# Gated attention block: the second norm's output is kept in natural layout, and turned and quantised from PSUM in the first barrier

## What is computed

```python
x = x + tanh(g_xattn) * attention(layernorm(x), ctx, ctx)      # causal scores, softmax over the query axis
y = layernorm(x)
s = sigmoid(clip_x) * max(abs(y)) / 127                        # one scale for the whole tensor
xq = clip(round(y / s), -128, 127) * s
gate, up = xq @ q(w_gate).T, xq @ q(w_up).T                    # 704 hidden columns, weights quantised by row
h = act_fake_quant(silu(gate) * up)                            # again one scale for the whole tensor
x = x + tanh(g_ffn) * (h @ q(w_down).T)
```

## Time and profile before

| | |
|---|---|
| median of 3 runs | 113.39 us (113.28 to 113.5) |
| profiled execution, its own time | 113.61 us |
| its span in the profile | 111.8 us |
| TensorE products, busy | 103.4 us, 93% |
| TensorE weight loads, busy | 79.7 us, 71% |
| VectorE, busy | 84.5 us, 76% |
| ScalarE, busy | 70.0 us, 63% |
| POOL, busy | 50.9 us, 46% |

### The profile page before, as it was taken

The page is one execution under the profiler, slowest core; times in us unless marked ns, Lnnn a source line. Parts: engine busy times, 40 slices in busy tenths (PEclk is TensorE's granted clock), DMA queues, the critical chain, the costliest instruction groups (busy, mean ns, idle before and its releaser), DMA issues.

```text
span 111.8 us, 1835 instructions
## 1 busy us (share of the span) xinstructions
PE 103.4 (93%) x614; PEld 79.7 (71%) x616; DVE 84.5 (76%) x209; ACT 70.0 (63%) x132; POOL 50.9 (46%) x85
## 2 busy tenths in 40 slices
PE   5979999999999999999999989999999799799960
PEld 2258888988889898898998977444444498677740
DVE  0274295697889959759559979659999997989992
ACT  0321252469864576645887978689888870999400
POOL 7214035073460815525066283046687631599910
PEclk9999999999999999999999999999999999999997
DMA  3998999998000000000000000000000000005555
GB/s 45 361 380 215 375 416 427 410 407 333 16 0 0 3 0 0 6 0 3 0 0 0 0 0 6 0 0 3 0 0 0 6 0 0 0 12 196 181 181 186
DMA packets 5513, 11.65 MB, mean 104 GB/s; under 512 B 640, under 2 KB 2688, under 8 KB 5504
## 3 DMA queue, kind: packets, MB, share of 16 engines
q1 hardware_dynamic: 4928, 10.75, 26.4%
q10 hardware_dynamic: 576, 0.79, 2.2%
HBM read 9.44 MB, written 2.10 MB: 103 GB/s over the span
## 4 chain that ended last, share of the span: by engine, by line
PE 51%; DVE 25%; DMA 6%; ACT 6%; POOL 4%; issue 4%; ACTq 1%; DVEq 0%; POOLq 0%
PE ps L450 13%; PE ps L472 11%; PE ps L498 9%; DVE hmax L1116 8%; DMA wvT<-in_wvT 6%; DVE ps L1148 4%; DVE xs L1152 4%; DVE shared L1111 3%; PE ps L508 2%; PE ps L510 2%; PE ps L509 2%; PE ps L658 2%; POOL shared L412 2%; PE ps L519 2%; POOL xn L401 2%
## 5 line engine op out<-in xcount | busy, mean ns | idle before, releaser
L658 PE MATMUL ps<-xq,wguT 128*128 128x512 bf16 x78 | 17.2, 379 | 0.1
L412 POOL TENSOR_TENSOR shared<-up_sb,silu 128x1024 f32<-128x1024 f32 x5 | 11.8, 2364 | 10.6 <-ACT up_sb L857 10.6
L658 PEld LDWEIGHTS ps<-xq,wguT 128*128 128x128 bf16 x80 | 7.8, 98 | 9.2 <-DVE shared L1111 0.2
L450 PE MATMUL ps<-wvT,shared 128*128 128x256 f32 x56 | 13.3, 380 | 0.2 <-DMA wvT<-in_wvT 0.2
L472 PE MATMUL ps<-shared,a_sb 128*128 128x256 f32 x56 | 13.2, 379 | 0.0
L1116 DVE TENSOR_REDUCE hmax<-shared 128x1 f32<-128x2048 f32 (+1 forms) x6 | 12.7, 2108 | 0.6 <-POOL shared L412 0.2
L362 POOL TENSOR_SCALAR var<-mv 128x2 f32<-128x2 f32 x8 | 1.5, 193 | 24.8 <-DVE mv L948 24.6
L852 ACT ACTIVATE silu<-ps,gu_scale 128x1024 f32<-128x1024 f32 x10 | 11.1, 1114 | 2.4 <-PE ps L658 2.4
L450 PEld LDWEIGHTS ps<-wvT,shared 128*128 128x128 f32 x56 | 10.6, 190 | 2.0 <-issue 0.6
L498 PE MATMUL ps<-uT,shared 128*128 128x256 f32 (+1 forms) x64 | 11.9, 329 | 0.0
L705 PE MATMUL ps<-wdT,hq 128*128 128x256 bf16 x80 | 11.0, 273 | 0.6 <-DVE hq L1163 0.5
(11 more groups left out here) (141 smaller groups left out, 217.4 us busy)
## 6 DMA issues: line engine op xcount, KB each, us to landing
shared<-in_xc SPq DMA_DIRECT2D x6, 512.0 KB, 10.8
out<-xs SPq DMA_DIRECT2D x7, 256.0 KB, 2.2
xs<-in_x SPq DMA_DIRECT2D x3, 512.0 KB, 8.4
shared<-in_wgu SPq DMA_DIRECT2D x3, 512.0 KB, 7.9
shared<-in_xc SPq DMA_DIRECT2D x4, 256.0 KB, 6.2
wd<-in_wd SPq DMA_DIRECT2D x1, 768.0 KB, 12.1
wq_sb<-in_wq ACTq DMA_DIRECT2D x1, 256.0 KB, 4.1
wk_sb<-in_wk SPq DMA_DIRECT2D x1, 256.0 KB, 3.9
```

What stands on the lines that cost most here:

```text
L412: nc.gpsimd.tensor_tensor(hid[:, 2 * i + 1, :], up_sb[i % 2][:], silu1[i % 2][:], ALU.mult).then_inc(hid_done[1], 1)
L450: last = nc.tensor.matmul(bank2(VB[b])[:, k, :], ctxT(b)[:, e, k * P:(k + 1) * P], weights[:, e, :], start=(e == 0), stop=(e == KT - 1))
L658: last = nc.tensor.matmul(bank(4 * half + 2 * g + c), wguT[:, i, g, k, :], xq[:, k, col:col + CH], start=(k == 0), stop=(k == KT - 1))
```

## The change

- The normalised second norm is kept whole in natural layout: `xn2` now has room for all 16 row tiles, and `xn2T` shrinks to two batches (512 columns).
- `transposes2` leaves the batch loop. Every batch is turned into a bank of its own, in the order 5, 0, 1, 2, 4, 3, 6, 7: batch 5 where it was, 0, 1, 2 and 4 behind the last attention, 3, 6 and 7 behind the spread of the maximum. The spread goes to bank RB in place of AT and waits for ScalarE's first copy out of RB.
- 9 keep-warm products before the spread become 2, and the 5 behind it go.
- ScalarE no longer copies turned batches in the loop. In the barrier it copies batches 4 and 5 to `xn2T`, and then makes integers of batches 1, 3, 6 and 7 from their banks. VectorE makes those of 0 and 2 from theirs. POOL makes those of 4 and 5 from `xn2T`, in one instruction of 128x1024.
- The number of clips and their shapes stay; their order against the integers changes.
- TensorE's half 1 of the first step waits for ScalarE's third conversion in place of the copies.

```diff
-WARM_BEFORE_MAX = 9
-WARM_AT_BARRIER = 5
+WARM_BEFORE_MAX = 2
-        xn2 = [sb(f"xn2_{p}", [P, QT, D]) for p in range(2)]
-        xn2T = sb("xn2T", [P, KT, B * S])
+        xn2 = sb("xn2", [P, NT, D])
+        xn2T = sb("xn2T", [P, KT, CH])
+        TB = (U, V0, V1, SC, X2, WT, AT, RB)
+        TURN_ORDER = (5, 0, 1, 2, 4, 3, 6, 7)
+        def turned(b):
+            return TURN_ORDER.index(b) + 1
...
# POOL, batches 6 and 7
-                pool.wait_ge(tr2_done, b - 1)
...
# POOL, behind gu_scale
+            pool.wait_ge(act_inv_done, 1)
+            pool.wait_ge(xn2T_ready, 2)
+            nc.gpsimd.tensor_scalar(xq_i16[:, :, 2 * CH:3 * CH], xn2T[:], act_inv[:, 0:1], 1.0, ALU.mult,
+                                    ALU.mult).then_inc(xq_int_pool, 1)
...
# TensorE
             def transposes2(b):
                 pe.wait_ge(xn2_ready, b + 1)
-                if b >= 1:
-                    pe.wait_ge(xn2T_ready, b)
...
                 attend(b)
-                if b >= 1:
-                    transposes2(b - 1)
...
-            pe.wait_ge(xn2T_ready, LAST - 2)
             turn_gate_up(2, X2)
             scores(LAST)
             attend(LAST - 1)
-            pe.wait_ge(wguT_last, 1)
+            pe.wait_ge(wguT_ready, 2)
             transposes2(LAST - 2)
...
+            for b in (0, 1, 2):
+                transposes2(b)
+            pe.wait_ge(wguT_last, 1)
+            transposes2(4)
             pe.wait_ge(x1_done, LAST)
             keep_warm(WARM_BEFORE_MAX, AT)
-            spread_max(0, AT)
-            pe.wait_ge(xn2T_ready, LAST - 1)
-            pe.wait_ge(wguT_ready, 2)
-            for b, bk in ((LAST - 1, X2), (LAST, WT)):
-                pe.wait_ge(xn2_ready, b + 1)
...
+            pe.wait_ge(x1_out, 1)
+            spread_max(0, RB)
             pe.wait_ge(x1_out, QT)
-            keep_warm(WARM_AT_BARRIER, SC)
+            transposes2(3)
+            transposes2(6)
+            pe.wait_ge(act_scale_done, 1)
+            transposes2(7)
...
                     if i == 0 and half == 1:
-                        pe.wait_ge(act_scale_done, 1)
-                        pe.wait_ge(xn2T_ready, LAST - 1)
+                        pe.wait_ge(xq_int_act, 3)
...
# ScalarE
-                if b >= 1:
-                    xn2T_out(b - 1)
...
-            xn2T_out(LAST - 2)
             for t, bk in enumerate((RB, SC)):
                 nc.scalar.copy(xs[:, NT - QT + t, :], bank(bk)[:, 0:D]).then_inc(x1_out, 1)
+            for n, b in enumerate((4, 5)):
+                act.wait_ge(tr2_done, turned(b))
+                nc.scalar.copy(xn2T[:, :, n * S:(n + 1) * S], bank2(TB[b])).then_inc(xn2T_ready, 1)
             act.wait_ge(act_inv_done, 1)
-            act.wait_ge(xn2T_ready, LAST - 1)
-            for c in range(2):
-                nc.scalar.activation(xq_i16[:, 1, c * CH:(c + 1) * CH], xn2T[:, 1, c * CH:(c + 1) * CH], ACT.Copy,
-                                     scale=act_inv[:, 0:1]).then_inc(xq_int_act, 1)
-            for b, bk in ((LAST - 1, X2), (LAST, WT)):
-                act.wait_ge(tr2_done, b + 1)
-                nc.scalar.activation(xq_i16[:, :, b * S:(b + 1) * S], bank2(bk), ACT.Copy,
+            for b in (1, 3, 6, 7):
+                act.wait_ge(tr2_done, turned(b))
+                nc.scalar.activation(xq_i16[:, :, b * S:(b + 1) * S], bank2(TB[b]), ACT.Copy,
                                      scale=act_inv[:, 0:1]).then_inc(xq_int_act, 1)
...
# VectorE
+            def input_ints(b):
+                dve.wait_ge(tr2_done, turned(b))
+                nc.vector.tensor_scalar(xq_i16[:, :, b * S:(b + 1) * S], bank2(TB[b]), act_inv[:, 0:1], None,
+                                        ALU.mult).then_inc(xq_int_dve, 1)
...
-            input_ints(0, 0)
-            input_ints(0, 1)
-            input_clip(0, 0)
-            input_clip(1, 0)
-            input_clip(0, 1)
-            input_clip(1, 1)
-            input_ints(both, 2)
-            input_clip(both, 2)
+            for c, b in enumerate((0, 2)):
+                input_ints(b)
+                dve.wait_ge(xq_int_dve, c + 1)
+                dve.wait_ge(xq_int_act, c + 1)
+                for k in range(KT):
+                    input_clip(k, c)
+            dve.wait_ge(xq_int_pool, 1)
+            input_clip(slice(0, KT), 2)
             dve.wait_ge(xq_int_act, 4)
-            input_clip(both, 3)
+            input_clip(slice(0, KT), 3)
```

More of the change, by code:

```diff
@@ L164, in inverse2, with xn2_rows @@
             return rstd2[:, b] if b < LAST - 1 else xfactor[:, B - 2 + QT * (b - B + 2):B - 2 + QT * (b - B + 3)]
+        def xn2_rows(b):
+            return xn2[:, QT * b:QT * (b + 1), :]
+        def turned(b):
+            return TURN_ORDER.index(b) + 1
         def ctxT(b):
@@ L265, in gated_block @@
         xq_int_dve = sem("xq_int_dve")
+        xq_int_pool = sem("xq_int_pool")
         xq_ready = sem("xq_ready")
@@ L374, in apply2 @@
                 for t in range(QT):
-                    last = nc.gpsimd.tensor_scalar(xn2[b % 2][:, t, :], xs[:, QT * b + t, :], neg_mean[:, b, t:t + 1],
+                    last = nc.gpsimd.tensor_scalar(xn2[:, QT * b + t, :], xs[:, QT * b + t, :], neg_mean[:, b, t:t + 1],
                                                    rstd2[:, b, t:t + 1], ALU.add, ALU.mult)
@@ L398, in _ @@
                 pool.wait_ge(neg_dev_done, QT * (b - LAST + 2))
-                pool.wait_ge(tr2_done, b - 1)
                 for t in range(QT):
-                    last = nc.gpsimd.tensor_scalar(xn2[b % 2][:, t, :], neg_dev[:, QT * (b - LAST + 1) + t, :],
+                    last = nc.gpsimd.tensor_scalar(xn2[:, QT * b + t, :], neg_dev[:, QT * (b - LAST + 1) + t, :],
                                                    inverse2(b)[:, t:t + 1], -1.0, ALU.mult, ALU.mult)
@@ L514, in transposes2 @@
                 pe.wait_ge(xn2_ready, b + 1)
-                if b >= 1:
-                    pe.wait_ge(xn2T_ready, b)
                 for e in range(KT):
                     for t in range(QT):
-                        last = nc.tensor.transpose(bank2(X2)[:, e, t * P:(t + 1) * P],
-                                                   xn2[b % 2][:, t, e * P:(e + 1) * P], ident[:])
+                        last = nc.tensor.transpose(bank2(TB[b])[:, e, t * P:(t + 1) * P],
+                                                   xn2[:, QT * b + t, e * P:(e + 1) * P], ident[:])
                 last.then_inc(tr2_done, 1)
@@ L1073, in global_scale @@
                 nc.vector.reciprocal(act_inv[:, n:n + 1], act_scale[:, n:n + 1]).then_inc(act_inv_done, 1)
[L1075 to L1081, removed]
+            global_scale(0, RB)
+            def input_ints(b):
+                dve.wait_ge(tr2_done, turned(b))
+                nc.vector.tensor_scalar(xq_i16[:, :, b * S:(b + 1) * S], bank2(TB[b]), act_inv[:, 0:1], None,
+                                        ALU.mult).then_inc(xq_int_dve, 1)
             def input_clip(k, c):
```

12 lines of the change are left out of this document (1 added, 11 removed).

## The result

The changed kernel takes 112.08 us (median of 4 runs, 111.74 to 112.14) against 113.34 us for the kernel before (4 runs). The ratio is 0.9883, with a 95% interval of 0.9866 to 0.9901: 1.3 us faster. The forecast was 111.5, 1.89 us faster; 0.6 us of the gain is missing.

A forecast was written before the change was run, and what follows sets the result against it. TensorE's queue was taken to bound the loop, with TensorE's queue and VectorE's integers and clips close together at the first barrier's end. -2.20 + 0.31 = -1.89 us from 113.39 gave 111.5 us; range 110.6 to 112.3.

The forecast's parts named there:

- Part 1: Batch loop: four turns leave TensorE's chain in each of five batches, 0.44 us each, 2.20 us gained.
- VectorE's margin of 0.01 us: Batch loop: VectorE needs 6.27 us per batch against the new period of 6.28, so it just fits.
- second rival: Batch loop: VectorE becomes the bound, 1.05 us of the gain is lost, 112.5 us; chance 0.1.
- Part 2: First barrier's first idle: 16 turns and 4 keep-warm halves replace 18 halves; cost 0, with 0.3 us of cover.
- Part 3: First barrier, behind the spread: three batches' turns and ScalarE's four conversions at 0.62 us each; nothing gained or lost.
- Part 4: First barrier's end: VectorE's conversions out of banks and POOL's conversion blocking its first clip make the first silu 0.31 us late.
- a slower POOL: First barrier: upper bound for POOL's 128x1024 conversion, 1.81 us, which gives 112.1 us.
- POOL does not hold VectorE up: First barrier: VectorE's clips do not collide with POOL's conversion; -2.52 us, 110.9 us; chance 0.25.
- its clock did not fall: First barrier: the rival had TensorE's clock dropping from 2.4 to 1.2 GHz in idle gaps, 114.9 us; chance 0.05.

The follow-up runs named there:

- experiment 1: Changed kernel with two keep-warm products (four halves) added behind the attention of batches 1 to 5, where the turns stood: 114.25 us, 2.17 over the changed kernel.
- experiments 2 and 3: Changed kernel with POOL's 128x1024 conversion given to VectorE, 111.31 us; made before POOL's small scale, 111.75 us; held until VectorE's first four clips are done, 112.19 us.
- experiment 4: Kernel before, without its five keep-warm products behind the last turns of the first barrier: 112.61 us, 0.9936 of before.

## Why the prediction was right, and which terms were off

**Part 1, five times 0.44 us: right.** All five, by the chain of waits, and experiment 1 gives 2.17 for putting them back. VectorE's margin of 0.01 us held: the periods that the chain shows are 6.28 each. One reading behind it was wrong, though. The prediction took 20.38 to 26.66 for the period of a batch without turns. But the link at 26.66 is that batch's own four turns, and the next batch starts at 27.09, so its period is 6.71 like the others':

```profile
27.09 1.31 PE ps L498 x8
```

No batch of the kernel before had run at 6.28. What the prediction held against its second rival, that one already did, was no evidence; that VectorE would keep up rested on the computed margin of 0.01 us alone.

**Part 2, covered: right.** From the last score maximum to the inverse scale it is 7.17 us in both traces, so 16 turns in place of 14 of the 18 keep-warm halves, and the new wait for ScalarE's copy, cost nothing.

**Part 3, ScalarE's conversions: right.** Four in 2.42 us, from 0.04 behind the inverse scale. They ended long before the silu.

**Part 4, the barrier's end: right in its mechanism, 0.33 us short.** The inverse scale stands at 67.35 in the prediction's times and at 64.49 in the trace after. With that 2.86 taken out, term by term:

| | forecast | measured |
|---|---|---|
| conversion of 512 columns out of a bank | 0.69 | 0.75, 0.74 |
| POOL's small scale | 0.19 | 0.28 |
| POOL's conversion starts | 67.82 | 67.79 |
| POOL's 1024 columns | 1.16 | 1.12 |
| last of the first two clips ends | 69.23 | 69.25 |
| fourth gate product starts | 70.40 | 70.52 |
| first silu | 70.69 | 71.02 |

The end of the blocked clips was forecast to within 0.02 us. The conversion was dearer than the row that it was taken from: 0.05 us of the 0.12 that had come together by the fourth product. The other 0.21 is a misread row. The prediction said of the twelve products that "the row counts eleven, one record is missing", but took 69.45 for the first of them. The missing record was the first one's. The timeline of the kernel before shows it by the weight load that belongs to it:

```profile
68.79 0.61 PE L445 MATMUL ps<-ones 128*128 128x128 f32 x4
...
69.13 0.42 PEld L658 LDWEIGHTS ps<-xq,wguT 128*128 128x128 bf16 x3
...
69.45 0.38 PE L658 MATMUL ps<-xq,wguT 128*128 128x512 bf16 x1
```

The loads took 0.1 us each, so the first one's product ran from 69.23 and 69.45 was the second. The silu comes 0.50 us behind the start of the fourth product, in both traces, and not 0.29. For the same reason the first gate product had waited 0.7 us behind the keep-warm products, not 0.9.

**The sum: one term was not in it.** The 0.37 us ahead of the product of step 1, 0.32 net of what the next step gives back, stands in no part of the prediction. That the time still fell inside the range, at 112.08 of 112.3, is luck in so far as its upper end was drawn for another case, a slower POOL. -1.89 + 0.33 + 0.32 = -1.24, against -1.26 by the medians.

**The rivals.** That POOL does not hold VectorE up fell with experiments 2 and 3. VectorE did not become the loop's bound. TensorE idled in the barrier as foreseen (2.11 us busy of 3.70 between 64.5 and 68.2) and its clock did not fall, here or in experiment 4. By the Trainium skill ("SBUF — State Buffer", the section SBUF: two separate sides) the loser of the shared ports waits for the winner's whole instruction. The first clip, timed back by 0.28 us from its end at 66.19, began 0.14 us before POOL's recorded end, so the trace agrees but for that overlap. By the same section of the Trainium skill only VectorE instructions in a mode that uses two SBUF ports, or with two inputs in SBUF, meet POOL there. A conversion whose input is a bank is neither, and POOL's small scale beside it took 0.28 instead of 0.47 (0.19 was forecast), so that agrees for the most part.

For the conversion out of a bank the estimate from the Trainium skill ("VectorE: DVE Perf Modes", the section on the TRN2 errata, 120 + 512 cycles) was 0.66 us. Measured were 0.75 and 0.74; the measurement decides.

## What to carry to other kernels

Work taken off the queue that is the chain pays in full, and what it is moved into decides what is kept: here 2.2 us were won in the loop and 0.64 paid in the barrier, which had 0.6 to win by dropping idle products alone. Do not put a POOL instruction over SBUF beside VectorE's SBUF conversions and clips when these are on the chain: give its work to VectorE behind the urgent ones (0.7 to 0.8 us here, part of it from the place of the product of step 1), or at least start it first (0.24 us here). How small VectorE's instruction is does not help: one of 2 columns waited 0.76 us for POOL. When a stage without any edit changes by a few tenths, compare the places of its instructions in the compiled program before looking for a cause in the edit.

## What the hardware showed that was not expected

- VectorE started one instruction 0.36 us late when it stood at place 189 of its program, and not at 188, 190 or 193; late in all seven kernels that had it at 189 and in none of the six others, and set and removed by instructions over 60 us ahead of it. One small instruction added in the source can leave the places of all behind it as they were.
- A VectorE instruction of 2 columns took 0.92 us beside POOL's 128x1024 product and ended 0.02 us behind it; ten like it without POOL beside them took 0.16 to 0.17 us. The length of a row in the timeline is in such a case mostly the wait.
- TensorE had up to 1.6 us of idle time out of 3.7 us in the barrier with the granted clock at 1.00 all the while; five keep-warm products of the kernel before bought nothing there.
